# A graph layer with 16 experts on one core: routing by block inside the gather loop, shorter VectorE instructions, and a tail whose second expert row is added by TensorE

## The chip, the cores and the metric

The kernel runs on one core of a Trainium2 chip. A core has five engines that run their own instruction streams and wait for each other by semaphores: TensorE (PE, matmuls; its weight loads are PEld), VectorE (DVE), ScalarE (ACT), GpSimd (POOL) and SyncE (SP, which here only issues DMAs). GpSimd issues the indirect DMAs, those that gather or scatter rows by a list of indices. The metric is the device time of the core in microseconds, lower is better. Before the change it is 911.88 us, the median of three runs of 909.67 to 912.08.

## What is computed

There are 3125 nodes with 256 features and 53125 edges sorted by destination (25000 drawn both ways, and a loop for each node). The reference, cut to what matters:

```python
h = layernorm(x)
agg = segment_sum(h[src], dst, n); deg = segment_sum(1, dst, n)
x = x + h @ W_self + (agg / max(deg, 1)) @ W_neigh + b
xt = layernorm(x)
v, e = top_k(xt @ gate_w + gate_b, 2)         # 16 experts
g = softmax(v)
moe = sum_k g[k] * (relu(xt @ w1[e_k] + b1[e_k]) @ w2[e_k] + b2[e_k])
out = x + layernorm(xt + moe) * gamma + beta
```

Each node picks two of the 16 experts, so 6250 pairs of node and expert are computed. fp32 values that TensorE multiplies are mostly split into two f16 halves (high and low), and three of the four products are taken.

## The kernel before

**Gather loop.** The layer norm h of all nodes is written to DRAM as rows of f16 halves (`h_tab`). The edges are 416 tiles of 128, taken in 26 loop iterations of 16 tiles, each of four quads. GpSimd gathers the source rows of each tile by one indirect DMA (L629) into a ring of 16 slots, and waits ahead of a quad until TensorE is through with the quad four earlier (`quads_done`). For each quad VectorE makes four one-hot matrices of destination against node in one instruction (`onehots`, L1149), and TensorE multiplies them with the gathered rows (L898, L899), two quads to a window of 128 nodes. ScalarE copies the sums out (`row_out`, L769), TensorE turns them (`turn_row`, L904, L905), and VectorE adds them into the node sums `AGG` (`add`, L1190).

**Blocks.** The nodes are 25 blocks of 125. Two iterations behind the edges (LAG = 2) one block per iteration goes through `mean` (L1198 to L1200), the products with W_self and W_neigh on TensorE (`x1_sum`), the layer norm on VectorE (`x1_norm`, L1212 to L1221; its reciprocal root is a chain of small instructions, L427 to L433, each waiting for the one before), the high half on ScalarE (`xt_high`, L759), turning on TensorE (L944), the gate's logits (`gate`), the two largest on VectorE (`gate_out`, L1231 to L1241), and the low half (`xt_low`, L1226). Also in each of the first 16 iterations one expert's W1 and W2 are split into f16 halves, 1024 columns an instruction (ScalarE L783 and L791, VectorE L1260 and L1275). Every engine's stream is written in one fixed order; nothing is scheduled at run time.

**Routing.** Once all blocks are through the loop, VectorE works over all of them at once (L1293 to L1333): one-hots of the chosen experts, a scan that counts each expert's pairs, and each pair's slot, item (tile of 128 pairs of one expert, 64 in all) and row in it; TensorE adds the counts over nodes (L985 to L987) and ScalarE takes the exponent of the softmax. In five chunks VectorE makes one-hots of the item (`eq`, L1338) and of the row (L1340), GpSimd multiplies `eq` by node number and by gate weight (L644, L645), and TensorE's fp32 products (L995) sum them to the lists `tok_of` and `meta_of` (L1347 to L1351).

**Experts.** Then the 64 items run in a pipeline of depth three: GpSimd fetches an item's 128 rows (L657), TensorE turns them (L1006), multiplies with W1 (L1018) and W2 (L1030), VectorE copies both weights to a fixed place (`load_w`, L1366, L1370) and takes the low half of the hidden layer (`split`, L1377), ScalarE copies, takes relu and high half, and scales by the gate weight (`weigh`, L839), and GpSimd scatters the rows to `z_tab` (L663).

**Tail.** In six chunks (2, 4, 6, 6, 4, 3 blocks), pieces of two blocks each: TensorE adds xt, by a product with a diagonal of the standard deviations made on ScalarE (L863, L1070), and b2 by the gate weights (L1071); VectorE adds the two expert rows (L1401), adds TensorE's sum (L1406), and takes moments (L1410, L1415) and centred rows (L1422); GpSimd takes the root (`row_scales`); the output goes out by an accumulating DMA. The last chunk takes its root and its last step (L1426) on VectorE.

## Time and profile before

| | us |
|---|---|
| timed runs | 912.08, 911.88, 909.67 |
| profiled execution, its own time | 907.16 |
| its span in the trace | 905.4 |
| GpSimd busy | 633.6 (70%) |
| TensorE busy | 541.3 (60%) |
| VectorE busy | 537.1 (59%) |
| ScalarE busy | 291.5 (32%) |
| mean granted clock of TensorE | 0.751 |

The span is the time from the first to the last record. The profile names an instruction group by its line, engine and operation, with the tiles it writes and reads (out<-in); "arena", "AGG" and "W" are large blocks of memory of which many tiles are parts, "PS" is the accumulation memory. Behind "|" stand the group's busy time, the mean ns of one, and the idle time of the engine just before them with what ended it; "issue" is time for which the profile shows no wait. The clock is the part of full speed that TensorE was granted; its two levels are 1.2 and 2.4 GHz, so 1.0 is 2.4 GHz.

Mean durations of VectorE's other instructions in the loop, of which the prediction adds up an iteration: an addition (L1190, 384 columns) 555 ns, the reciprocal of `mean` (L1199) 939 ns, its product (L1200) 425 ns, the low half (L1226) 417 ns, the layer norm's wide instructions (L1212, L1215, L1219) 419 to 428 ns and its small ones (L427 to L433) 154 to 164 ns, and those of `gate_out` 168 to 185 ns.

### The profile page before, as it was taken

To read this page: it belongs to the slowest core of one execution; us is meant where nothing else is said; L and a number is where in the kernel's file an instruction comes from. 1 tells how busy PE (TensorE), PEld (TensorE's weight loads), DVE (VectorE), ACT (ScalarE), POOL (GpSimd) and SP (SyncE) were. 2 spreads that over 40 slices of the span, in tenths; PEclk is the share of its full clock that TensorE was granted. 3 is DMA by queue.
4 is the path that set the end of the run, shared out by engine and by line. 5 is a ranking of instruction groups with operands and counts; after the bars stand their busy time and mean duration, and the time that the engine had idled before them with its cause. 6 is when DMAs were issued, how large, how long until landed. Compare 5 with 4: busy or idle time off the path is not lost.

```text
span 905.4 us, 15122 instructions
## 1 busy us (share of the span) xinstructions
PE 541.3 (60%) x4348; PEld 435.3 (48%) x4348; DVE 537.1 (59%) x1386; ACT 291.5 (32%) x688; POOL 633.6 (70%) x657
## 2 busy tenths in 40 slices
PE   0034565565565664646556556632789999999720
PEld 0022443444343443434434444421689999998610
DVE  7622356666556666564554554468577777777296
ACT  5311111112211121100110000010188999988621
POOL 6377777777777777777777777505757777776265
PEclk9995566656666667576676677555799999999965
DMA  8544555566555555544444444310133223222897
GB/s 192 166 151 147 156 166 178 166 185 186 178 176 172 169 174 168 155 130 122 128 128 128 122 127 127 108 30 22 35 87 93 91 90 93 72 88 65 190 228 115
DMA packets 65021, 120.09 MB, mean 133 GB/s; under 512 B 11645, under 2 KB 39469, under 8 KB 64970
## 3 DMA queue, kind: packets, MB, share of 16 engines
q0 software_dynamic: 29088, 72.17, 28.4%
q1 hardware_dynamic: 35734, 46.86, 18.4%
q8 instruction: 26, 0.43, 0.2%
q10 hardware_dynamic: 148, 0.43, 0.2%
q14 instruction: 25, 0.20, 0.1%
HBM read 100.21 MB, written 21.19 MB: 134 GB/s over the span
## 4 chain that ended last, share of the span: by engine, by line
POOL 45%; PE 23%; issue 15%; DMA 8%; DVE 7%; SPq 1%; ACT 0%; DVEq 0%; ACTq 0%; POOLq 0%
POOL arena L629 42%; PE PS L1018 9%; PE PS L1030 9%; DMA arena<-h_tab,arena 4%; PE PS L1006 1%; DMA W<-z_tab 1%; DMA arena<-xh_tab,tok_of 1%; PE PS L995 1%; PE PS L898 1%; DMA W<-in_x 1%; DVE W L1422 1%; PE PS L899 1%; POOL AGG L644 1%; DVE W L1406 1%; DMA z_tab<-arena,meta_of 1%
## 5 line engine op out<-in xcount | busy, mean ns | idle before, releaser
L629 POOL DMA_INDIRECT arena<-h_tab,arena x416 | 412.7, 992 | 138.6 <-issue 124.3
L898 PE MATMUL PS<-arena 128*128 128x257 f16 x416 | 142.4, 358 | 214.6 <-DMA arena<-h_tab,arena 214.4
L898 PEld LDWEIGHTS PS<-arena 128*128 128x128 f16 x416 | 51.2, 123 | 253.6 <-issue 183.6
L899 PE MATMUL PS<-arena 128*128 128x256 f16 x416 | 145.3, 364 | 0.0
L1190 DVE TENSOR_TENSOR AGG<-AGG,PS 128x384 f32 x52 | 28.9, 555 | 124.5 <-PE PS L905 118.9
L1018 PE MATMUL PS<-arena,AGG 128*128 128x128 f16 x1536 | 97.5, 221 | 1.6 <-DVE AGG L1366 1.6
L1149 DVE TENSOR_TENSOR arena<-iota,arena 128x512 f16<-128x512 f16 x104 | 70.2, 690 | 45.3 <-PE PS L899 37.0
L1030 PE MATMUL PS<-AGG,arena 128*128 128x256 f16 x768 | 95.8, 273 | 0.2 <-DVE arena L1377 0.2
L759 ACT ACTIVATE arena<-arena 125x256 f16<-125x256 f32 x25 | 10.4, 417 | 256.3 <-DVE arena L1219 256.3
L769 ACT ACTIVATE arena<-PS 128x257 f32<-128x257 f32 x52 | 19.8, 380 | 226.9 <-PE PS L899 226.9
L663 POOL DMA_INDIRECT z_tab<-arena,meta_of x64 | 69.7, 1090 | 31.7 <-issue 19.0
L1018 PEld LDWEIGHTS PS<-arena,AGG 128*128 128x128 f16 x1536 | 89.8, 99 | 1.8 <-DVE AGG L1366 1.8
L657 POOL DMA_INDIRECT arena<-xh_tab,tok_of x64 | 74.9, 1170 | 22.5 <-ACT arena L839 13.4
L1030 PEld LDWEIGHTS PS<-AGG,arena 128*128 128x128 f16 x768 | 72.5, 98 | 9.2 <-issue 0.5
L823 ACT ACTIVATE arena<-PS,arena 128x128 f32<-128x128 f32 x256 | 73.0, 368 | 5.9 <-PE PS L1018 3.6
L1377 DVE TENSOR_TENSOR arena<-arena 128x512 f16<-128x512 f32 x64 | 44.3, 692 | 46.6 <-ACT arena L832 46.6
L899 PEld LDWEIGHTS PS<-arena 128*128 128x128 f16 x416 | 51.4, 123 | 13.4
L832 ACT ACTIVATE arena<-arena 128x512 f16<-128x512 f32 x64 | 40.3, 630 | 16.0 <-PE PS L1030 15.8
L1366 DVE COPY AGG<-W 128x2048 f16 x64 | 44.7, 699 | 0.3 <-issue 0.3
L1370 DVE COPY AGG<-W 128x2048 f16 x64 | 44.9, 702 | 0.0
L815 ACT ACTIVATE arena<-PS 128x512 f16<-128x512 f16 x64 | 37.6, 587 | 5.5 <-PE PS L1006 5.5
L944 PE MATMUL PS<-ident,arena 125*128 125x125 f32 x50 | 16.7, 438 | 37.3 <-DVE arena L1219 37.2
(208 smaller groups left out, 971.4 us busy)
## 6 DMA issues: line engine op xcount, KB each, us to landing
W<-in_L_ffn_w SPq DMA_DIRECT2D x31, 512.0 KB, 4.0
arena<-h_tab,arena POOLq DMA_INDIRECT x416, 3.0
arena<-h_tab SPq DMA_DIRECT2D x25, 125.0 KB
arena<-in_x SPq DMA_DIRECT2D x25, 125.0 KB
out<-arena SPq DMA_DIRECT2D x25, 125.0 KB
xh_tab<-arena SPq DMA_DIRECT2D x25, 125.0 KB
W<-z_tab SPq DMA_DIRECT2D x2, 1344.0 KB
W<-z_tab SPq DMA_DIRECT2D x2, 896.0 KB
```

Of the source, the lines that this page charges most:

```text
L629: g.indirect_dma_start(msg[:, s, u, 0:2 * D], None, h_tab[:, :], bass.IndirectOffsetOnAxis(ap=srcT[:, t:t + 1], axis=0)).then_inc(gathered ...
L657: g.indirect_dma_start(xsr[:, n % 4, :].bitcast(f16), None, xh_tab[:, :], bass.IndirectOffsetOnAxis(ap=tok_of[:, n:n + 1], axis=0)).then_i ...
L663: g.indirect_dma_start(z_tab[:, :], bass.IndirectOffsetOnAxis(ap=meta_of[:, n, 0:1].bitcast(i32), axis=0), yo[:, n % 4, :], None, bounds_c ...
L823: ins = a.activation(hr[:, s % 2, c * P:(c + 1) * P], p_h[s % 2][:, c * P:(c + 1) * P], ACT.Relu, bias=b1e[:, s % 2, c:c + 1], scale=1.0 / ...
L898: t.matmul(p, oh[:, h, u, :], msg[:, s, u, D:2 * D + 1], start=first, stop=False)
L899: return t.matmul(p[:, 0:D], oh[:, h, u, :], msg[:, s, u, 0:D], start=False, stop=last)
L1018: ins = t.matmul(p_h[s % 2][:, c * P:(c + 1) * P], w1e[:, s % 2, wa, k, c * P:(c + 1) * P], xT[:, s % 2, xa, k, :], start=(y == 0), stop=( ...
L1030: ins = t.matmul(p_y[s % 2], h[:, s % 2, c * P:(c + 1) * P], w2e[:, s, wa, c, :], start=(y == 0), stop=(y == len(terms) - 1))
L1149: v.tensor_tensor(oh[:, h, :, :], iota16[:, :].unsqueeze(1).to_broadcast([P, QT, P]), relT[:, bass.ds(TPR * r + QT * h, QT)].unsqueeze(2). ...
L1366: v.tensor_copy(w1e[:, s % 2, :, :, :].rearrange("p a k f -> p (a k f)"), W1[:, bass.ds(e, 1), :, :, :].rearrange("p e a k f -> p (e a k f ...
L1370: v.tensor_copy(w2e[:, s, :, :, :].rearrange("p a c d -> p (a c d)"), W2[:, bass.ds(e, 1), :, :, :].rearrange("p e a c d -> p (e a c d)")) ...
L1377: v.tensor_tensor(hl[:, s % 2, :], hr[:, s % 2, :], hh[:, s % 2, :], ALU.subtract).then_inc(h_split, 1)
```

## The change

1. **Short instructions.** The one-hots of a quad are four instructions of 128 columns with the destination as a scalar per row. The weights' low halves are made in four pieces each.
2. **Routing by block.** In the loop, behind `gate_out`, a new `pick` makes the one-hots of the block's two experts; TensorE (`place`) counts each pair's place among its expert's pairs, from the block and a running count; a new `place_rows` on VectorE makes of it the row one-hots of the block's pairs, once times the place of the node within its block (`row_tok`) and once times the block's number (`row_blk`), in f16. The loop is staged anew (`place_rows` three iterations behind the mean), the root of `x1_norm` is shortened to nine linked instructions on a column (`rsqrt_column`), and TensorE's node products are parted in two (own, neighbours).
3. **The last iteration** is written out apart and the last blocks have second buffers for the rows, turned rows and logits, and block 23 goes through its norm, gate and pick between the last quads' steps.
4. **Routing's end.** With the tiles of each expert known, the pairs' items are found by one product and one sum over the experts (L1485, L1486); five `eq` of 640 elements follow; TensorE makes the lists by 200 f16 products (two for each half block) and VectorE puts both together (L1500 to L1505). GpSimd has no part in it.
5. **Gate weights.** The rows that go to `z_tab` are not scaled any more. All factors are left as a ratio e1 to the first expert's weight; the norm's eps is scaled along (`epsr`). `gate_rows` (VectorE, ahead of the fourth item's weight copy) and `gate_low` make the factors for b2 and xt while the experts run.
6. **The tail.** VectorE makes the diagonals of xt once TensorE is through with the experts, ScalarE those of the ratio (`diag_r`), and TensorE adds the second expert's rows by fp32 products with them (`second_expert`), with the products of xt and b2 six pieces ahead. VectorE's addition of the two rows goes.

The order of VectorE's stream at three places. First, behind the last block's mean; before (block 24, numbered from 0):

```order
L1200 TENSOR_TENSOR arena<-AGG,arena 128x250 [waits deg_step]
L1226 TENSOR_TENSOR arena<-arena 125x256 [waits xt_hi]
L1285 TENSOR_SCALAR AGG<-iota 128x25 [waits mean_made]
L1286 MEMSET AGG 125x400
L1287 MEMSET AGG 125x16 [waits dve_step]
L1231 TENSOR_TENSOR lg<-PS,gb_b 125x16 [waits logits,dve_step]
L1235 MAX m<-lg 125x8 [waits logits_out,top_out]
L1238 MAX_INDEX i<-m,lg 125x8 [waits top_step]
L1239 COPY val<-m 125x2
L1241 CAST idxf<-i 125x2 [waits top_step]
L1212 SCALAR_TENSOR_TENSOR arena<-PS,arena 125x256 [waits xx_stored,hxx_loaded,x1_summed]
```
and with the change:

```order
L1308 TENSOR_TENSOR arena<-AGG,arena 128x250 [waits deg_step]
L1380 TENSOR_TENSOR arena<-AGG,PS 125x32 [waits ohs_made,pos_made]
L1382 TENSOR_TENSOR cum<-cum,ohs 125x16 [waits place_step]
L1383 TENSOR_REDUCE arena<-arena 125x2
L1384 CAST arena<-arena 125x2 [waits place_step]
L1385 TENSOR_SCALAR arena<-arena 125x2 [waits place_step]
L1386 CAST AGG<-arena 125x2 [waits place_step]
L1389 TENSOR_SCALAR arena<-arena 125x1 [waits place_step,cols_made]
L1390 SCALAR_TENSOR_TENSOR arena<-AGG,arena 125x2 [waits place_step]
L1393 TENSOR_SCALAR AGG<-iota,arena,tok 125x128 [waits place_step]
L1393 TENSOR_SCALAR AGG<-iota,arena,tok 125x128
L1396 TENSOR_SCALAR AGG<-iota,arena 125x128 x2
```
Before, the low half and the first rows of the routing over all blocks follow, and then the gate of block 23. Now the 11 instructions of `place_rows` for block 22 stand between the mean and the norm of block 24, and block 23's gate is ahead of the mean.

Second, in the chunks of the routing's end, `eq` and row one-hots before (L1338, L1340):

```order
L1340 TENSOR_TENSOR arena<-iota,AGG 125x1280
L1338 TENSOR_TENSOR AGG<-iota,AGG 125x640 [waits pv_made]
L1340 TENSOR_TENSOR arena<-iota,AGG 125x1280
L1338 TENSOR_TENSOR AGG<-iota,AGG 125x640 [waits pv_made]
L1340 TENSOR_TENSOR arena<-iota,AGG 125x1280
L1347 TENSOR_SCALAR tok_of<-PS 128x64 [waits chunk_done]
L1348 TENSOR_SCALAR tok_of<-tok_of 128x64 [waits dve_step]
```
and with the change (L1490 is `eq`):

```order
L1490 TENSOR_TENSOR arena<-iota,arena 125x640 [waits dve_step]
L1493 TENSOR_SCALAR arena<-arena,iotap 128x16
L1494 TENSOR_REDUCE arena<-arena 128x1 [waits dve_step]
L1495 TENSOR_SCALAR arena<-arena 128x1 [waits dve_step]
L1490 TENSOR_TENSOR arena<-iota,arena 125x640 x3
L1498 CAST items<-PS 1x64 [waits item_T]
L1490 TENSOR_TENSOR arena<-iota,arena 125x640
L1500 COPY arena<-PS 128x64 [waits chunk_done]
L1501 SCALAR_TENSOR_TENSOR arena<-PS,arena 128x64 [waits dve_step]
L1502 TENSOR_SCALAR tok_of<-arena 128x64 [waits dve_step]
```
The waits for GpSimd's products (`pv_made`) and the row one-hots of 1280 elements are gone; the small steps behind the sums are more.

Third, in the experts, from the second item's `split` on; before:

```order
L1377 TENSOR_TENSOR arena<-arena 128x512 [waits hi_split]
L1362 TENSOR_LOAD items
L1362 ISA x2
L1365 ISA [waits relu_done,l1_done]
L1365 COPY arena<-b1T 128x4
L1366 ISA
L1366 COPY AGG<-W 128x2048
```
and with the change, where `gate_rows` (L1513 to L1522) comes ahead of the fourth item's weights (L1537):

```order
L1552 TENSOR_TENSOR arena<-arena 128x512 [waits hi_split]
L1513 MEMSET arena 125x1200 [waits xh_stored,xx_stored,ratio_made]
L1514 TENSOR_SCALAR AGG<-AGG 125x25x16
L1515 SCALAR_TENSOR_TENSOR AGG<-AGG,ratio 125x25x16
L1517 TENSOR_TENSOR arena<-AGG 125x25x16 [waits gates_summed]
L1518 TENSOR_SCALAR epsr<-ratio 125x25
L1519 TENSOR_TENSOR rstds<-rstds,epsr 125x25 [waits gates_summed]
L1520 TENSOR_SCALAR arena<-rstds 125x25 [waits gates_summed]
L1522 SCALAR_TENSOR_TENSOR epsr<-epsr 125x25 [waits g3_zeroed]
L1537 TENSOR_LOAD items
```
Eight instructions have been put ahead of the copies of the fourth item's weights, and the first of them waits for ScalarE's ratio and for stores.

The diff, cut to its core:

```diff
+        def rsqrt_column(v, link, var, vs, t, y):
+
+            link(v.scalar_tensor_tensor(vs, quads[0:BT, :], var, quads_eps[0:BT, :], ALU.mult, ALU.add))
+            link(v.tensor_scalar(t.bitcast(i32), vs[:, 0:1].bitcast(i32), 1, None, ALU.logical_shift_right))
+            link(v.tensor_scalar(y.bitcast(i32), t.bitcast(i32), -1.0, float(0x5F3759DF) - 2.0 ** 31, ALU.mult, ALU.add))
+            for c in range(3):
+                link(v.scalar_tensor_tensor(t, y, vs[:, c:c + 1], y, ALU.mult, ALU.mult))
+                link(v.scalar_tensor_tensor(y, t, 3.0, y, ALU.subtract, ALU.mult))
...
-                g.tensor_tensor(pv[c % 2][:, :, 0, :], eq[c % 2], tok1[:, js].unsqueeze(2).to_broadcast([BT, CH, NITEM]), ALU.mult).then_inc(pv_made, 1)
-                g.tensor_tensor(pv[c % 2][:, :, 1, :], eq[c % 2], wts[:, js].unsqueeze(2).to_broadcast([BT, CH, NITEM]), ALU.mult).then_inc(pv_made, 1)
...
+            def place(j):
+
+                pe.wait_ge(ohs_made, j + 1)
+                pe.wait_ge(cum_made, j + 1)
+                t.matmul(p_pos[in_end(j)], lower16[:, :], ohs[is_last(j)][:, :], start=True, stop=False)
+                t.matmul(p_pos[in_end(j)], ones16[0:BT, 0:BT], cum[:, :], start=False, stop=True).then_inc(pos_made, 1)
...
-                pe.wait_ge(oh_row_made, c + 1)
-                pe.wait_ge(pv_made, 2 * (c + 1))
-                for j in range(CH):
-                    ins = t.matmul(p_meta, oh_row[:, c * CH + j, :], pv[c % 2][:, j, :, :],
-                                   start=(c == 0 and j == 0), stop=(c == NG - 1 and j == CH - 1))
+                pe.wait_ge(eq_made, c + 1)
+                for j in range(c * CH, (c + 1) * CH):
+                    b, k = divmod(j, 2)
+                    t.matmul(p_tok, row_tok[:, b, k, :], eq[:, j, :], start=(j == 0), stop=(j == BK - 1))
+                    ins = t.matmul(p_blk, row_blk[:, b, k, :], eq[:, j, :], start=(j == 0), stop=(j == BK - 1))
...
+            def second_expert(i):
+
+                lo, hi = PIECES[i]
+                pe.wait_ge(diag_r_made, i + 1)
+                pe.wait_ge(z_loaded[CHUNK_OF[i]], 2 * DMA)
+                for b in range(lo, hi):
+                    ins = t.matmul(p_sum[i % 8][:, b - lo, :], diag_r[:, b, :], Z[0:BT, b, 1, :], start=False, stop=(b == hi - 1))
                 ins.then_inc(p_made, 1)
+
+            for i in range(AHEAD):
+                residual(i)
+            for i in range(len(PIECES)):
+                second_expert(i)
+                if i + AHEAD < len(PIECES):
+                    residual(i + AHEAD)
...
-                v.tensor_tensor(oh[:, h, :, :], iota16[:, :].unsqueeze(1).to_broadcast([P, QT, P]),
-                                relT[:, bass.ds(TPR * r + QT * h, QT)].unsqueeze(2).to_broadcast([P, QT, P]),
-                                ALU.is_equal).then_inc(signal, 1)
+                for u in range(QT):
+                    ins = v.tensor_scalar(oh[:, h, u, :], iota16[:, :], relT[:, bass.ds(TPR * r + QT * h + u, 1)], None, ALU.is_equal)
+                ins.then_inc(signal, 1)
...
+                link(v.tensor_tensor(o, iota16[0:BT, 0:NEXP].unsqueeze(1).to_broadcast([BT, 2, NEXP]),
+                                     idx2[:, :].unsqueeze(2).to_broadcast([BT, 2, NEXP]), ALU.is_equal), alone=True)
+                v.tensor_tensor(ohs[is_last(j)][:, :], o[:, 0, :], o[:, 1, :], ALU.add).then_inc(ohs_made, 1)
...
+            def place_rows(j):
+
+                link, n = counted_link(dve, place_step, PLACE_STEPS * j)
+                o = oh2[:, bass.ds(j, 1), :].rearrange("p b (k e) -> p (b k) e", k=2)
+                t2 = tiles[:, bass.ds(j, 1), :].rearrange("p b k -> p (b k)")
+                dve.wait_ge(pos_made, j + 1)
+                dve.wait_ge(ohs_made, j + 1)
+                link(v.tensor_tensor(picked[:, :, :], o, p_pos[in_end(j)].unsqueeze(1).to_broadcast([BT, 2, NEXP]), ALU.mult), alone=True)
+                if not is_last(j):
+                    v.tensor_tensor(cum[:, :], cum[:, :], ohs[0][:, :], ALU.add).then_inc(cum_made, 1)
+                link(v.tensor_reduce(pos2[:, :], picked[:, :, :], AX.X, ALU.add))
+                link(v.tensor_copy(tile2[:, :], pos2[:, :]))
+                link(v.tensor_scalar(tile2[:, :], tile2[:, :], P.bit_length() - 1, None, ALU.logical_shift_right))
+                link(v.tensor_copy(t2, tile2[:, :]))
+                dve.wait_ge(cols_made, j + 1)
+                carry(dve)
+                link(v.tensor_scalar(block1[:, :], block1[:, :], 1.0, None, ALU.add))
+                link(v.scalar_tensor_tensor(row2[:, :], t2, -float(P), pos2[:, :], ALU.mult, ALU.add), alone=True)
+                assert n[0] == PLACE_STEPS
+                for k in range(2):
+                    v.tensor_scalar(row_tok[:, bass.ds(j, 1), k, :].rearrange("p b c -> p (b c)"), iota16[0:BT, :],
+                                    row2[:, k:k + 1], tok2[:, k:k + 1], ALU.is_equal, ALU.mult)
+                for k in range(2):
+                    ins = v.tensor_scalar(row_blk[:, bass.ds(j, 1), k, :].rearrange("p b c -> p (b c)"), iota16[0:BT, :],
+                                          row2[:, k:k + 1], block1[:, 0:1], ALU.is_equal, ALU.mult)
+                ins.then_inc(cols_made, 1)
...
-                        v.scalar_tensor_tensor(w[:, 1, :], wstg1, WS1, w[:, 0, :], ALU.mult, ALU.subtract).then_inc(w1_lo, 1)
+                        for c in range(4):
+                            cs = slice(c * KC * F // 4, (c + 1) * KC * F // 4)
+                            ins = v.scalar_tensor_tensor(w[:, 1, cs], wstg1[:, cs], WS1, w[:, 0, cs], ALU.mult, ALU.subtract)
...
+            xt_low(NB - 3)
+            x1_norm(NB - 2)
+            place_rows(NB - 4)
+            add(LAST, 0)
+            gate_out(NB - 3)
+            pick(NB - 3)
+            last_base = row_base(2 * LAST + 1)
+            add(LAST, 1, last_base)
             dve.wait_ge(adds_done, ER + 2)
             mean(NB - 1)
+            place_rows(NB - 3)
+            x1_norm(NB - 1)
             xt_low(NB - 2)
...
+            gate_out(NB - 2)
+            pick(NB - 2)
+            gate_out(NB - 1)
+            pick(NB - 1)
+            place_rows(NB - 2)
+            xt_low(NB - 1)
+            dve.wait_ge(top_out, 2 * NB + 2)
...
+            link(v.tensor_tensor(at_e, ohf, tile0[0:BT, :].unsqueeze(1).unsqueeze(1).to_broadcast([BT, NB, 2, NEXP]), ALU.mult))
+            link(v.tensor_reduce(itemf.rearrange("p (b k) -> p b k", k=2), at_e, AX.X, ALU.add))
...
+                v.memset(G3, 0.0).then_inc(g3_zeroed, 1)
+                v.tensor_scalar(pairs[:, :, 0, :], ohf[:, :, 0, :], WS2, None, ALU.mult)
+                link(v.scalar_tensor_tensor(pairs[:, :, 1, :], ohf[:, :, 1, :], WS2, ratio[:, :].unsqueeze(2).to_broadcast([BT, NB, NEXP]),
+                                            ALU.mult, ALU.mult))
+                v.tensor_tensor(gates[:, :, 0:NEXP], pairs[:, :, 0, :], pairs[:, :, 1, :], ALU.add)
+                link(v.tensor_scalar(epsr[:, :], ratio[:, :], 1.0, WS2, ALU.add, ALU.mult))
+                link(v.tensor_tensor(rstds[:, :], rstds[:, :], epsr[:, :], ALU.mult))
+                v.tensor_scalar(gates[:, :, NEXP], rstds[:, :], -1.0, None, ALU.mult)
...
+            for lo, hi in PIECES:
+                for b in range(lo, hi):
+                    ins = v.tensor_scalar(diag[:, b, :], ident[0:BT, 0:BT], rstds[:, b:b + 1], None, ALU.mult)
...
-                link(v.tensor_tensor(z[:, :, 0, :], z[:, :, 0, :], z[:, :, 1, :], ALU.add))
...
```
## Rows read from the trace of the kernel before

**Rows 1.** Stretches; from:to, length, busy of PE, PEld, DVE, ACT, POOL (instructions), clock, DMA, GB/s.
```profile
41.86:582.90 541.04, 301.81 (x1512) 217.21 (x1513) 283.11 (x823) 78.52 (x152) 412.68 (x416) 0.67 0.52 153
582.90:652.80 69.90, 31.39 (x166) 26.73 (x167) 48.14 (x115) 5.37 (x11) 27.89 (x19) 0.62 0.09 26
652.80:844.00 191.20, 187.54 (x2558) 175.87 (x2556) 134.36 (x253) 167.08 (x446) 139.75 (x123) 0.99 0.31 88
```

**Rows 2.** Costliest groups of the page, the gather.
```profile
L629 POOL DMA_INDIRECT arena<-h_tab,arena x416 | 412.7, 992 | 138.6 <-issue 124.3
```

**Rows 3.** The gather's line: ns least/median/most, first and last start.
```profile
L629 POOL DMA_INDIRECT arena<-h_tab,arena x416: 942/946/1897, 41.9 to 580.0; - x139
```

**Rows 4.** Timeline in the gather; start us, duration us, engine, line.
```profile
453.00 1.30 DVE L1149 TENSOR_TENSOR arena<-iota,arena 128x512 f16<-128x512 f16 x2 [0.34 <-issue]
453.12 1.39 POOL L629 DMA_INDIRECT arena<-h_tab,arena  x1 [0.30 <-issue]
```

**Rows 5.** Timeline from the last gather to the first fetch.
```profile
580.03 0.95 POOL L629 DMA_INDIRECT arena<-h_tab,arena  x1 [0.30 <-issue]
...
582.90 0.38 PE L898 MATMUL PS<-arena 128*128 128x257 f16 x1 [1.82 <-DMA arena<-h_tab,arena]
...
608.93 0.98 DVE L1294 TENSOR_TENSOR AGG<-iota,idxf 125x800 f32<-125x800 f16 x1
...
620.21 0.82 DVE L1338 TENSOR_TENSOR AGG<-iota,AGG 125x640 f32<-125x640 f16 x1
...
647.80 0.99 POOL L657 DMA_INDIRECT arena<-xh_tab,tok_of  x1 [1.10 <-DVE tok_of L1348]
```

**Rows 6.** Groups by line, VectorE, 41.86 to 582.9 us.
```profile
L1149 DVE TENSOR_TENSOR arena<-iota,arena 128x512 f16<-128x512 f16 x102 | 68.9, 691 | 43.4 <-PE PS L899 37.0 <-issue 5.5
...
L1275 DVE SCALAR_TENSOR_TENSOR W<-W 128x1024 f32 (+1 forms) x15 | 18.3, 1218 | 0.0
...
L1221 DVE TENSOR_TENSOR arena<-arena,beta_b 125x256 f32<-125x256 f32 x23 | 9.9, 430 | 0.8
...
L1198 DVE TENSOR_SCALAR arena<-AGG 128x125 f32 (+1 forms) x24 | 6.0, 250 | 3.9 <-DVE AGG L1190 3.8
```

**Rows 7.** Timeline of VectorE, last block.
```profile
595.35 0.23 DVE L1198 TENSOR_SCALAR arena<-AGG 128x125 f32<-128x125 f32 x1
...
596.70 0.42 DVE L1200 TENSOR_TENSOR arena<-AGG,arena 128x250 f32<-128x250 f32 x1
...
601.13 0.43 DVE L1212 SCALAR_TENSOR_TENSOR arena<-PS,arena 125x256 f32<-125x256 f32 x1
...
604.81 0.15 DVE L1218 COPY rstds<-arena 125x1 f32<-125x1 f32 x1
605.00 0.41 DVE L1219 TENSOR_SCALAR arena<-arena 125x256 f32<-125x256 f32 x1
```

**Rows 8.** Timeline in and behind the experts.
```profile
659.17 1.01 PE L1018 MATMUL PS<-arena,AGG 128*128 128x128 f16 x15 [1.59 <-DVE AGG L1366]
...
699.27 1.23 POOL L657 DMA_INDIRECT arena<-xh_tab,tok_of  x1 [0.31 <-ACT arena L839]
...
699.68 0.69 DVE L1366 COPY AGG<-W 128x2048 f16 x1
...
843.86 1.54 PE L1053 MATMUL PS<-ident,AGG 125*96 125x125 f16 x25
```

**Rows 9.** Groups by line, VectorE, 851 to 905.4 us.
```profile
L1401 DVE TENSOR_TENSOR W<-W 125x1024 f32<-125x1024 f32 (+3 forms) x6 | 7.6, 1265 | 14.1 <-DMA W<-z_tab 14.1
```

**Rows 10.** Timeline of the tail, TensorE and VectorE.
```profile
864.73 1.06 PE L1070 MATMUL PS<-W,AGG 125*125 125x256 f32 x2
...
866.64 1.76 DVE L1401 TENSOR_TENSOR W<-W 125x1536 f32<-125x1536 f32 x1 [0.16 <-DMA W<-z_tab]
...
875.37 1.75 DVE L1401 TENSOR_TENSOR W<-W 125x1536 f32<-125x1536 f32 x1
```

**Rows 11.** Groups by line, VectorE, 653 to 844 us.
```profile
L1370 DVE COPY AGG<-W 128x2048 f16 x63 | 44.1, 700 | 0.0
```

579 lines of the change are left out of this document (332 added, 247 removed).

## The prediction

> **What bounds the kernel now.** I read the stretches first, then the costliest groups, then the order of time at each seam. The stretches [rows 1] part the span of 905.4 us. From 41.9 to 582.9 us the edges are gathered: GpSimd is busy 412.7 of 541 us, no other engine over 302. From 582.9 to 652.8 the routing runs, 69.9 us with every engine mostly idle: a chain from engine to engine. From 652.8 to 844.0 the 64 items of the experts run with TensorE busy 187.5 of 191.2 us at the high clock. What is left, 61.4 us, is the tail (DMA, then VectorE).
>
> In the gather GpSimd is the bound by itself: 416 gathers, least 942 ns, median 946, mean 992, and gaps put down to "issue" of 124.3 us, 0.30 each [rows 2 to 4]. An undisturbed gather is 0.945 + 0.300 = 1.245 us, a loop iteration of 16 is 19.9 us, and 415 steps are 517 us; the rest up to the last start at 580.03 [rows 5] is 416 x (0.992 - 0.946) = 19.1 us of lengthened gathers, plus 2. What lengthens them stands in [rows 4]: a gather that begins at 453.12, while VectorE's one-hot of 453.00 is running, takes 1.39 us: it waits until about 0.12 us before that instruction's end at 453.69. The row of 453.00 holds two one-hots back to back; the gather waits only for the first, so the wait ends between them.
>
> **The gather, part by part.** The one-hot of 512 columns (102 x 0.691 us, two tensor inputs) becomes four of 128 with a column scalar; a weight split of 1024 columns (30 x 1.218, two lines with x15 each) becomes four of 256 [rows 6]. A gather that starts inside an instruction of length L waits on average (L - 0.12)^2 / 2L. Before: 70 us of one-hots meet 70/1.3 = 54 starts x 0.235 = 13; 37 us of splits meet 28 x 0.495 = 14; together 27, where the rows show 19, so I scale by 0.7. After: the nearest row for 128 columns is 0.25 us (x24), for 256 columns 0.43 (x23) [rows 6]: 104 us at most in 80 starts x 0.034 = 2.7, and 42 us in 33 x 0.11 = 3.7, scaled 4.5. The new per-block instructions are as short; I add 1.5. So 6 of 19 stay: **13 us gained** (5 to 19, no less than the scaling doubled, no more than all of it).
>
> This holds only while VectorE keeps up. A full iteration on it, by start-to-start spacing: four one-hot groups 2.8 (4 x 0.17 each), two additions 1.6, mean 1.8 (595.35 to 597.12 [rows 7]), low half 0.4, layer norm 4.1 (601.13 to 605.41 is 4.3, less three linked steps of 0.19, as between 604.81 and 605.00, plus 0.43 for the beta row [rows 6, 7]), gate and pick 1.9, place_rows 2.3 (seven linked steps, four instructions of at most 0.25), weight splits 8 x 0.34 = 2.7: 17.6 of 19.9 us, and without weights 15. Before it was busy 283 of 541 us [rows 1], which leaves out the gaps of its linked steps. TensorE's new waits (place for the pick) stand a whole iteration behind in the loop, and GpSimd waits for a quad only four quads later, some 9 us of slack. So the new work is hidden there; without that cover it would be 2.7 us x 20 iterations.
>
> **The bridge.** Four pieces, from the last gather's landing (582.90, TensorE's first matmul on it [rows 5]) to the first fetch (647.80).
> 1. To the last mean: before 596.70 + 0.42 - 582.90 = 14.2 us [rows 7]. After, VectorE's queue in the last iteration decides. From about 8.3 us after the first of its four landings (TensorE is through with own and neighbour products and the second quad at 8.7) it has: norm of block 22 4.1, one-hot 0.7, gate and pick 1.6, low half 0.4, norm of 23 4.1, place_rows 2.1, addition 0.8, gate and pick 1.6, addition 0.9, mean 1.8 = 18.1, so the mean is there at 26.4 to 27.2, and the last landing is at 15: 12.0. Gain 2.
> 2. Mean to normalized rows of block 24: before 597.12 to 605.41 = 8.3 [rows 7]. After place_rows of 22 (2.1) and a norm of 3.5: 5.8. Gain 2.5.
> 3. From there to the first routing instruction over all blocks at 608.93 it was 3.5. Now: row tail 0.6, two low halves 0.8, two gates and picks 3.1, the difference 0.2, two place_rows 4.2 = 8.9. Loss 5.4. Then 608.93 to 620.21 was 11.3 [rows 5]; its successor is five small steps at 0.21, two of 800 elements at 0.98 (the row of 608.93 has 800) and one of 0.2: 3.3. Gain 8.
> 4. The five chunks: 620.21 to 647.80 = 27.6 us [rows 5], in which GpSimd's products and VectorE's comparisons take turns. After, GpSimd has none of it; the five comparisons of 640 elements take at most 0.82 each, as the one of 620.21 did before GpSimd began, and TensorE's 200 matmuls follow. I count 100 pairs as two instructions that hide each other's loads half: 0.062 us for one at the high clock (25 in 1.54 us [rows 8]), twice that at the low one, so 6.2 to 25 us; TensorE starts low (0.62 in this stretch [rows 1]). I take 9 for all of them, plus 0.7 ahead and 1.0 of small steps behind: 10.7. Gain 17 (2 to 20).
> Sum: 2 + 2.5 - 5.4 + 8 + 17 = 24; I take **23.5 us** (bounds 9 to 29). The 5.0 us from fetch to first matmul stay.
>
> **The experts.** TensorE, the bound, has the same instructions. New is gate_rows in VectorE's queue ahead of the weight copy for item 3: a memset of 1200 words (1.3 us by the 0.82 of 640 elements), three of 400 elements (0.5 each) and four small ones (0.2): 3.6 us. VectorE has 134 us of work in 191 [rows 1] and catches up later, but at the start TensorE already waits for just such a copy (659.17, 1.59 us [rows 8]). I put 3 of it on the path; ScalarE's two copies (1.0 us), on an engine busy 167 of 191 us [rows 1], add 0.5: **3.5 lost** (1 to 6).
>
> **The tail.** VectorE's additions of the second row go: 6, 7.6 us busy [rows 9]; from 866.64 on it was the bound [rows 10]. In their place each piece of two blocks needs two fp32 products on TensorE before VectorE may add: 0.85 us a block at the low clock (1.06 with the overlap of its two passes [rows 10]), half at the high one, and the residual of six pieces ahead (0.55, or 1.06, a block) stands between them. VectorE needs 2.3 us per piece (a chunk of three from 866.64 to 875.37 is 8.73, less the 1.76 that go [rows 10]), TensorE 2.0 at the high clock and 4.1 at the low one, until the residuals are through. Walking the chunks gives 2 us gained at the high and 5 lost at the low clock; the last chunk's own steps stay. I take **1 gained** (7.6 gained to 5 lost). The 25 diagonals (4.8 us on VectorE) lie under the wait for the z table (most of 14.1 us [rows 9]).
>
> **Sum.** -13 - 23.5 + 3.5 - 1 = -34.0. The profiled execution took 907.16 us (span 905.4), so 873.2 by its own time; the median of the timed runs is 4.7 above it, and by that 877.9. I forecast **878**.
>
> **Rivals.**
> A. The seam is longer than my walk: TensorE's small matmuls at the low clock throughout take 20 instead of 9 us, or the last iteration's queue slips by one norm. For it: every engine's work there is in one order with waits in both directions, and the clock was 0.62 [rows 1]. Against: TensorE has work without gaps in the chunks, and such work ran at the high clock in the experts [rows 1]. Price 11: 889.
> B. All of it pays: 18 of the gather's 19 us, chunks in 7.5, the tail's 7.6 less 1. For it: two-input instructions are the only ones that I find before long gathers. Price: -5 - 1.5 - 5.6: 866.
> C. **VectorE becomes the bound of the gather** (slower). Place: the loop's 24 new short instructions. If each has to wait for GpSimd's port and stands 0.36 us instead of 0.17, the iteration needs 17.6 + 24 x 0.19 = 22.2 us. It decides from 19.9 on, and the gain of the other parts (21 us) is gone when 20 iterations exceed that by 2.0 each, 21.9. At 22.2 the loop is 46 us over its floor, where before it was 19: 911.9 - 21 + 27 = 918. Against it: VectorE's copies of 2048 columns average 0.700 us x63 [rows 11] while GpSimd's descriptors are written in 73% of the time (139.75 of 191.2 us [rows 1]), and the gather at 699.27 is what waits (1.23 us) behind the copy of 699.68 [rows 8].
> The Trainium skill, "SBUF — State Buffer", section "Who interferes with whom", speaks for C: a one-source instruction such as tensor_scalar or copy can enter a two-port mode and then it and a GpSimd instruction block each other, whoever starts first, whereas tensor_tensor only meets GpSimd's reads. By that rule the change swaps a weak contender for a strong one. The trace agrees that the copy holds GpSimd up in mid-instruction, and shows no wait of VectorE.
> D. The short instructions free nothing, the lengthened gathers staying at 19 us: 891 with the rest as forecast. Against: the wait ends with the first of two back-to-back instructions [rows 4].
>
> **Chances.** Forecast (870 to 885) 0.55; A 0.15; B 0.14; D 0.08; C 0.06; the rest, a miss in both gather and bridge that ends within a few us of no change, 0.02. Range 864 to 894: it leaves out C, the far end of A and the far end of B; the forecast's own range is 870 to 885. Within 0.3% (2.7 us) is about what a measurement cannot tell from no change. Faster 0.92, same 0.02, slower 0.06.
>
> **What would show it.** Gather: mean of the 416 near 0.96 us, last start near 567, few over 1.2. Bridge: 46 us from last landing to first expert matmul, with the last mean 12 us in, and GpSimd idle. Experts: one TensorE wait of about 3 us near the third item, then 2.9 us each. Tail: no addition of the second row, VectorE waiting on TensorE in several pieces. It would be wrong if GpSimd waits for TensorE in the loop (C), if the gathers keep their 0.992 mean (D), or if the small matmuls take over 15 us (A).

## The result, and the profile after

The changed kernel takes 888.80 us, the median of 4 runs (886.31 to 889.21), against 911.98 us of the kernel before (909.67 to 912.34, 4 runs): a ratio of 0.9752, 95% interval 0.9734 to 0.9769. That is 23.2 us faster, where 33.9 were forecast. The profiled execution took 888.89 us, its span is 887.1 us, 18.3 under the span before; the profiled execution before was 4.8 us under its own median, and in which stretch these 4.8 us lie no trace shows.

By stretch, each from the two traces (forecast in the last column):

| stretch | before | after | change | forecast |
|---|---|---|---|---|
| start to first gather | 41.86 | 43.29 | +1.4 | 0 |
| first to last gather start | 538.17 | 535.88 | -2.3 | -13 |
| last gather to first fetch | 67.77 | 46.83 | -20.9 | -23.5 |
| first fetch to first W1 product | 5.02 | 4.95 | -0.1 | 0 |
| first W1 product to end of last W2 product | 191.20 | 195.08 | +3.9 | +3.5 |
| from there to the end | 61.3 | 61.1 | -0.3 | -1 |

The first row is no part of the change: kernels with the same start had their first gather at 41.3 to 42.5 us. The stretches of the changed kernel (from:to, length, busy time and instructions of PE, PEld, DVE, ACT and POOL, clock, DMA share, GB/s) stand against [rows 1]:

```profile
43.29:582.10 538.81, 292.66 (x1551) 227.88 (x1552) 344.00 (x1450) 78.34 (x151) 410.39 (x416) 0.71 0.51 154
582.10:630.95 48.85, 21.72 (x177) 17.86 (x178) 35.12 (x140) 4.60 (x10) 4.03 (x4) 0.53 0.12 35
630.95:826.02 195.07, 188.68 (x2557) 175.65 (x2556) 137.59 (x262) 162.11 (x448) 140.81 (x124) 0.99 0.29 87
```

GpSimd is almost idle in the second (4.03 of 48.9 us, was 27.9 of 69.9), and in the first it is as busy as before: 410.4 against 412.7 us. The gather's line, which answers to [rows 3], says where that comes from (ns least/median/most):

```profile
L677 POOL DMA_INDIRECT arena<-h_tab,arena x416: 942/946/3239, 43.3 to 579.2; - x139
```

The median is the same, but the longest gather now takes 3.24 us, before 1.90. Of the 416, six take over 1.5 us. Summed over all gathers, what each takes over 0.945 us is 19.6 us before and 17.3 after. Sorted by what VectorE was doing when a lengthened gather began (the instruction begun last, if it was still running), in us, with the gathers lengthened by over 0.02 us and all that began there:

| VectorE at the gather's start | before | after |
|---|---|---|
| one-hot, two inputs (before) or scalar (after) | 10.25 (38 of 52) | 0.24 (7 of 54) |
| weights' low halves | 8.1 (18 of 29) | 13.0 (22 of 26) |
| other two-input instructions | 0.6 | 3.4 |

Of the 14 that began in a two-input one-hot and were not lengthened, 11 began in its last 0.15 us, where the gather gets in at once; so did all 11 not lengthened in the low halves before. So the one-hots gave what was forecast and more, and the weights' low halves, cut in four, and the other two-input instructions took it back. The timeline shows how; the first of the six long gathers (start us, duration us):

```profile
67.39 0.95 POOL L677 DMA_INDIRECT arena<-h_tab,arena  x1 [0.30 <-issue]
67.70 0.24 DVE L1253 TENSOR_SCALAR arena<-iota,arena 128x128 f16<-128x128 f16 x1
67.87 1.42 DVE L1426 SCALAR_TENSOR_TENSOR W<-W 128x256 f16<-128x256 f32 x4
68.65 2.80 POOL L677 DMA_INDIRECT arena<-h_tab,arena  x1 [0.30 <-issue]
69.21 1.42 DVE L1432 SCALAR_TENSOR_TENSOR W<-W 128x256 f16<-128x256 f32 x4
71.75 0.95 POOL L677 DMA_INDIRECT arena<-h_tab,arena  x1 [0.30 <-issue]
```

The gather of 68.65 begins while the third of the first four pieces runs. If it waited for that piece alone it would be lengthened by 0.2 us, as with the one-hots in [rows 4]. It is held through the rest of L1426 and all four pieces of L1432, to 70.51, 0.12 us before their end at 70.63, and then takes its 0.945: 2.80 us. The eight pieces follow each other every 0.335 us; the waits for ScalarE's high halves, ahead of the first and the fifth, had long been met and held nothing up. The six long gathers stand in iterations 0 to 4 and 15, the ones whose weight part is written out for one iteration; in the ten iterations that run as a loop (5 to 14) the gathers beside the same pieces are lengthened by 0.27 us at most. Four of the kernels below leave this part of the loop as it is (`gate_rows`, the last quad, both of the tail), and their traces say the same: in each of iterations 0 to 4 a gather is held until 0.12 us before the row's end, 25 of 25 with the changed kernel, and in 50 loop iterations none is. A gather that began 0.08 us ahead of the first piece, in the last scalar one-hot, was held longest (with `gate_rows` moved):

```profile
156.58 0.74 DVE L1253 TENSOR_SCALAR arena<-iota,arena 128x128 f16<-128x128 f16 x4 [2.19 <-PE PS L935]
157.16 3.66 POOL L677 DMA_INDIRECT arena<-h_tab,arena  x1 [0.30 <-issue]
157.24 1.42 DVE L1426 SCALAR_TENSOR_TENSOR W<-W 128x256 f16<-128x256 f32 x4
158.58 1.42 DVE L1432 SCALAR_TENSOR_TENSOR W<-W 128x256 f16<-128x256 f32 x4
```

Iteration 15, with one row of four pieces, is mixed: held to the row's end in three of the five, but in the kernel with the last quad ahead a gather that began in the first piece got in at that piece's end:

```profile
380.95 1.43 DVE L1439 SCALAR_TENSOR_TENSOR W<-W 128x256 f16<-128x256 f32 x4
381.08 1.11 POOL L677 DMA_INDIRECT arena<-h_tab,arena  x1 [0.30 <-issue]
```

### The profile page after: what moved, and what is told of

The parts are those of the page before. It is cut to its first block, busy times and chain, and to the rows that moved or that the text cites. A ratio compares the mean times of both kernels' runs of the same rounds, so it can differ in the third digit from the quotient of the medians.

```text
span 887.1 us, 16659 instructions
## 1 busy us (share of the span) xinstructions
PE 535.8 (60%) x4447; PEld 446.4 (50%) x4447; DVE 586.1 (66%) x2080; ACT 285.5 (32%) x688; POOL 602.5 (68%) x643
## 3 DMA queue, kind: packets, MB, share of 16 engines
q1 hardware_dynamic: 35734, 46.86, 18.3%
## 4 chain that ended last, share of the span: by engine, by line
POOL 45%; PE 20%; issue 17%; DVE 8%; DMA 8%; SPq 1%; ACT 0%; DVEq 0%; ACTq 0%; POOLq 0%
POOL arena L677 43%; PE PS L1103 8%; PE PS L1115 8%; DMA arena<-h_tab,arena 2%; DMA arena<-xh_tab,tok_of 2%; DMA W<-z_tab 1%; PE PS L1091 1%; DMA W<-in_x 1%; POOL arena L685 1%; DVE W L1604 1%; DMA z_tab<-arena,meta_of 1%; PE PS L934 1%; DVE arena L1592 1%; PE PS L935 1%; POOL W L638 1%
## 5 line engine op out<-in xcount | busy, mean ns | idle before, releaser
L677 POOL DMA_INDIRECT arena<-h_tab,arena x416 | 410.4, 987 | 138.5 <-issue 124.0
L934 PE MATMUL PS<-arena 128*128 128x257 f16 x416 | 145.8, 364 | 249.2 <-DMA arena<-h_tab,arena 249.1
L1253 DVE TENSOR_SCALAR arena<-iota,arena 128x128 f16<-128x128 f16 x416 | 80.2, 272 | 114.3 <-PE PS L935 111.4
L935 PE MATMUL PS<-arena 128*128 128x256 f16 x416 | 148.5, 370 | 0.0
L685 POOL DMA_INDIRECT arena<-xh_tab,tok_of x64 | 72.7, 1136 | 67.6 <-DVE tok_of L1503 45.9
L691 POOL DMA_INDIRECT z_tab<-arena,meta_of x64 | 73.9, 1154 | 34.0 <-ACT arena L869 18.6
L792 ACT ACTIVATE arena<-PS 128x250 f32<-128x250 f32 x25 | 9.5, 378 | 179.0 <-PE PS L991 179.0
L971 PE MATMUL PS<-ws,arena 128*125 128x256 f16 x150 | 35.5, 404 | 0.0
```

The costliest lines, as they stand in the source:

```text
L677: g.indirect_dma_start(msg[:, s, u, 0:2 * D], None, h_tab[:, :], bass.IndirectOffsetOnAxis(ap=srcT[:, t:t + 1], axis=0)).then_inc(gathered ...
L685: g.indirect_dma_start(xsr[:, n % 4, :].bitcast(f16), None, xh_tab[:, :], bass.IndirectOffsetOnAxis(ap=tok_of[:, n:n + 1], axis=0)).then_i ...
L691: g.indirect_dma_start(z_tab[:, :], bass.IndirectOffsetOnAxis(ap=meta_of[:, n:n + 1], axis=0), yo[:, n % 4, :], None, bounds_check=2 * N - ...
L934: t.matmul(p, oh[:, h, u, :], msg[:, s, u, D:2 * D + 1], start=first, stop=False)
L935: return t.matmul(p[:, 0:D], oh[:, h, u, :], msg[:, s, u, 0:D], start=False, stop=last)
L1253: ins = v.tensor_scalar(oh[:, h, u, :], iota16[:, :], relT[:, bass.ds(TPR * r + QT * h + u, 1)], None, ALU.is_equal)
```

## The experiments

Each kernel was timed in turns with the kernel before, and not with the changed kernel. Before's time was 910.97 us beside whole instructions, linked pieces and the two forms of two-input one-hots, 908.17 beside one wait ahead, `gate_rows`, the last quad and the tail by chunk, and 910.05 beside the other four; beside the changed kernel it was 911.98. The totals are set against the changed kernel's 888.80 all the same, so a difference of under about 4 us between two of them shows nothing by itself, and the stretches of the traces decide. The ratio to the kernel before, 0.9752 for the changed kernel, stands with each. "Lengthening" is the sum over the 416 gathers of what each took over 0.945 us; "loop" is first to last gather start.

### The rows of pieces: four kernels

**Whole instructions again.**

```diff
-for c in range(4):
-    ins = v.scalar_tensor_tensor(w[:, 1, cs], wstg1[:, cs], WS1, w[:, 0, cs], ALU.mult, ALU.subtract)
-ins.then_inc(w1_lo, 1)
+v.scalar_tensor_tensor(w[:, 1, :], wstg1, WS1, w[:, 0, :], ALU.mult, ALU.subtract).then_inc(w1_lo, 1)
```

(and so for W2.)

> The changed kernel, with the low halves of the weights made by one instruction of 1024 columns again instead of four of 256. Theory run: VectorE instructions with two tensor inputs that follow each other without a semaphore wait between them hold the gathers up until the last of them is nearly done, so four pieces in a row count as one long instruction (12 gathers of the changed kernel's trace, 1.3 to 2.3 us longer each, 12 us in all, stand behind such rows of pieces). Then one long instruction costs the same as four pieces: 887 to 891 us, and again some 12 gathers of over 2 us. Theory length: each instruction holds by itself, so the pieces did help and the long ones must come from elsewhere; then this is 5 to 8 us slower, 894 to 897 us.

Measured: 887.16 us (883.49 to 888.84), ratio 0.9722, lengthening 17.1, loop 535.7. The longest gather takes 3.18 us; ten take over 1.5. Cutting an instruction of 1024 columns in four gained nothing in sum, as theory run has it: the two whole instructions, now one behind the other, also hold as one in four of the first five iterations. (The changed kernel's trace has six gathers held by a row, 10.6 us together, and not the 12 that theory run sets out from.) The sum hides two parts. In the ten loop iterations, where nothing holds as one, the pieces lengthen gathers by 2.4 us and the whole instructions by 5.0; in the six written out it is 10.6 against 8.2.

**Pieces linked by waits.**

```diff
+plink, _ = counted_link(dve, piece_step, 6 * i)
 for c in range(4):
     ins = v.scalar_tensor_tensor(w[:, 1, cs], wstg1[:, cs], WS1, w[:, 0, cs], ALU.mult, ALU.subtract)
+    if c < 3:
+        plink(ins)
```

> The changed kernel, with each piece of a weight's low half waiting by a semaphore for the piece before it. Theory run: the row of pieces is broken, a gather waits for one piece of 0.4 us at most, and of the 13 us of lengthening behind pieces (12 gathers) 2 to 3 stay: 878 to 881 us, no gather over 1.5 us behind a split. Theory length: nothing changes, 889, or a little slower by the added waits of VectorE.

Measured: 877.02 us (874.66 to 878.72), ratio 0.9618, 11.8 us under the changed kernel; lengthening 5.6, loop 524.2, 11.7 shorter:

```profile
L678 POOL DMA_INDIRECT arena<-h_tab,arena x416: 942/946/1337, 42.4 to 566.6; - x139
```

With a wait of each piece for the one before it no gather takes over 1.34 us. The whole difference in time is the difference in lengthening.

**One wait ahead of the pieces.** The pieces are as in the changed kernel; VectorE only waits for its own last one-hot first.

```diff
 if weights == "both":
+    dve.wait_ge(oh_ready, QR * i + 6)
     dve.wait_ge(w1_hi, i + 1)
```

> The changed kernel, with one wait of VectorE for its own last one-hot ahead of the first piece of the weights' low halves; the pieces themselves follow each other without waits as in the changed kernel. Theory entered (in the changed kernel the row of pieces stands behind one-hots with a column scalar; with two-input one-hots in their place no gather was held over 1.5 us, so it is the passage from the one-hots into the pieces that leaves the hold in place): the wait breaks the passage, no gather over 1.5 us, 877 to 880 us. Theory pieces (a row of pieces holds whatever stands ahead of it): as the changed kernel, 886 to 890 us, 6 or more gathers over 1.5 us.

Measured: 879.58 us (879.21 to 880.29), ratio 0.9682, lengthening 6.2, loop 524.8, no gather over 1.28 us. The same place in its timeline:

```profile
64.85 0.66 DVE L1253 TENSOR_SCALAR arena<-iota,arena 128x128 f16<-128x128 f16 x3
65.54 1.43 DVE L1427 SCALAR_TENSOR_TENSOR W<-W 128x256 f16<-128x256 f32 x4
65.79 1.00 POOL L677 DMA_INDIRECT arena<-h_tab,arena  x1 [0.30 <-issue]
66.89 1.42 DVE L1433 SCALAR_TENSOR_TENSOR W<-W 128x256 f16<-128x256 f32 x4
67.09 1.03 POOL L677 DMA_INDIRECT arena<-h_tab,arena  x1 [0.30 <-issue]
```

Two gathers begin inside rows of pieces that run as closely as before, and each gets in at the end of the piece that it met (1.00 and 1.03 us). So theory pieces, by which a row of pieces holds whatever stands ahead of it, fell. What counts is how VectorE comes into the row. It takes a wait for VectorE's own last instruction: the wait for ScalarE's high half stood ahead of the row in the changed kernel too and did not help. In iterations 0 to 4 the row starts 0.03 us behind the last one-hot's end with its own wait, and 0.08 us ahead of that end without it.

Where in the row a gather begins does not explain it. In iterations 0 to 4 the held ones of the changed kernel began 0.34 to 1.04 us behind the row's start; with the wait they began at 0.22 to 0.25 and 1.09, with the four two-input one-hots below at 0.39 to 1.01, and none was held past its piece.

**Whole instructions with the wait ahead** (both edits above).

> The changed kernel, with the weights' low halves in one instruction of 1024 columns each and the wait ahead of them. Theory entered (the hold that outlasts an instruction is what the wait mends; the length of each instruction then counts by itself): a gather that starts in one is held at most 1.1 us, some 10 to 20 of the 31 instructions are hit for 0.5 us each, so 5 to 9 us over the kernel with pieces and the wait (879.6): 884 to 888. If the wait alone is all that matters: 879 to 881.

Measured: 885.40 us (883.56 to 889.22), ratio 0.9728, lengthening 13.8, longest gather 1.98. The hold is back to one instruction (1.98 is 1.04 + 0.945), and with the way in mended, length does count: 13.8 against 6.2 us. So with the wait the pieces are worth 7.6 us (the loop is 532.4 us against 524.8), where without it they were worth nothing in sum.

### The one-hots: three kernels

**One instruction with two inputs again.**

```diff
-for u in range(QT):
-    ins = v.tensor_scalar(oh[:, h, u, :], iota16[:, :], relT[:, bass.ds(TPR * r + QT * h + u, 1)], None, ALU.is_equal)
-ins.then_inc(signal, 1)
+v.tensor_tensor(oh[:, h, :, :], iota16[:, :].unsqueeze(1).to_broadcast([P, QT, P]),
+                relT[:, bass.ds(TPR * r + QT * h, QT)].unsqueeze(2).to_broadcast([P, QT, P]),
+                ALU.is_equal).then_inc(signal, 1)
```

> The changed kernel, with the one-hots of a quad in one instruction of 512 columns with two tensor inputs again. Both theories: the gathers that start inside it are lengthened as in the kernel before (35 gathers, 10.2 us there): 897 to 901 us, gather mean 1.00 to 1.02 us. A third theory, that the form of the one-hots never mattered and the order of the stream is what counts, gives 889.

Measured: 890.58 us (885.90 to 894.37), ratio 0.9768, lengthening 19.1: only 1.8 slower, where both theories had 8 or more. The sum is nearly the same, its parts are not: 51 gathers behind one-hots make 14.4 us, and the low halves make 2.7 us, with no gather over 1.5. The long holds are gone without any edit of the pieces. This miss led to the experiment with the wait ahead.

**Four instructions with two inputs.**

```diff
-    ins = v.tensor_scalar(oh[:, h, u, :], iota16[:, :], relT[:, bass.ds(TPR * r + QT * h + u, 1)], None, ALU.is_equal)
+    ins = v.tensor_tensor(oh[:, h, u, :], iota16[:, :],
+                          relT[:, bass.ds(TPR * r + QT * h + u, 1)].to_broadcast([P, P]), ALU.is_equal)
```

> The changed kernel, with the four one-hots of a quad as four instructions of 128 columns, but with two tensor inputs each (tensor against tensor, the scalar column stretched) and no wait between them. Theory run: they hold as one instruction of 0.7 us, as slow as the single one of 512 columns (897 to 901 us). Theory length: four short holds of 0.17 us, 1 to 3 us over the changed kernel: 890 to 892 us. Theory scalar form irrelevant: 889.

Measured: 880.12 us (877.72 to 882.35), ratio 0.9653, 8.7 faster than with the scalar form, which no theory had. Lengthening is 9.1: 36 of 72 gathers begun in one-hots make 4.0 us, against 0.24 for the scalar form, and the low halves make 2.8 against 13.0. Four short two-input instructions without a wait do not hold as one, so theory run is wrong in its general form. The three forms also part the one-hots' gain: 14.4 us in one instruction, 4.0 in four with two inputs, 0.24 in four with a scalar. So length gave most of it and the form the rest. Its timeline at the low halves:

```profile
86.88 1.42 DVE L1427 SCALAR_TENSOR_TENSOR W<-W 128x256 f16<-128x256 f32 x4
87.68 1.10 POOL L677 DMA_INDIRECT arena<-h_tab,arena  x1 [0.30 <-issue]
88.22 1.42 DVE L1433 SCALAR_TENSOR_TENSOR W<-W 128x256 f16<-128x256 f32 x4
89.08 1.04 POOL L677 DMA_INDIRECT arena<-h_tab,arena  x1 [0.30 <-issue]
```

The same rows of pieces, entered from two-input one-hots with no wait, let each gather in at the next boundary.

**The kernel before with scalar one-hots only** (the first diff of this group, the other way, in the kernel before).

> The kernel before, with only the one-hots changed: four instructions of 128 columns with a column scalar instead of one of 512 with two tensor inputs. In its trace the gathers behind one-hots are lengthened by some 10 us. Theory length: nearly all of this goes, 8 to 10 us below the kernel before in the same rounds. Theory entered: the one-hots stand ahead of the low half of W1 here too, and the hold passes on into it in some iterations, so 4 to 8 us below.

Measured: 904.19 us (901.70 to 906.07) against 910.05, ratio 0.9930 (0.9909 to 0.9951): 5.9 us faster. Lengthening 14.8, 14 gathers over 1.5 us, the longest 1.92, all of them beside an instruction of 1024 columns. Gathers begun in one-hots make 0.3 us (9 of 51 lengthened) against 10.25, but those begun in the low halves 13.3 (26 of 31) against 8.1 (18 of 29). The gain is within theory entered's numbers, but not by its mechanism: no gather there is held past one instruction. The low halves of W1 and W2 stand apart in it, and only two of its iterations are written out, so it could hardly show the long hold. About as many gathers meet the low halves as before, but earlier in them: 11 of the 29 had begun in the last 0.15 us, now 5 of 31. Before, a gather held by the one-hot ahead put the next one just at the low half's end, so in 10 of 16 iterations:

```profile
193.03 1.42 POOL L629 DMA_INDIRECT arena<-h_tab,arena  x1 [0.30 <-issue]
193.55 1.22 DVE L1260 SCALAR_TENSOR_TENSOR W<-W 128x1024 f32 x1
194.75 0.95 POOL L629 DMA_INDIRECT arena<-h_tab,arena  x1 [0.30 <-issue]
```

So a hold that is taken away moves the gathers behind it, and some of them meet the next long instruction worse.

### The three other terms

**gate_rows where VectorE is idle.**

```diff
-dve_step_of(n)
-if n == -1:
-    gate_rows()
+if n == -2:
+    run_item(load_w, n, 3, None)
+    gate_rows()
+    run_item(split, n, 2, None)
+else:
+    dve_step_of(n)
```

> The changed kernel, with gate_rows put between the second item's weight copies and the first item's split, where VectorE stands idle for 4.63 us, instead of ahead of the fourth item's weight copies. Theory queue (the 3.9 us that the experts grew come from TensorE waiting for copies queued behind gate_rows): TensorE's wait of 2.71 us goes, first up product to last down product 195.1 us becomes 191.2 to 192, total 3 to 4 us less: 885. Theory other (the growth is from ScalarE's two copies or from GpSimd): at most 1 us less.

Measured: 882.91 us (881.87 to 888.30), ratio 0.9740, experts 190.54 us (195.08). In the changed kernel TensorE stands twice for weight copies in the first items:

```profile
637.29 1.51 PE L1103 MATMUL PS<-arena,AGG 128*128 128x128 f16 x24 [1.27 <-DVE AGG L1541]
...
643.07 1.51 PE L1103 MATMUL PS<-arena,AGG 128*128 128x128 f16 x24 [2.71 <-DVE AGG L1541]
```

and in this one only once, then 2.9 us an item from the third:

```profile
635.46 1.51 PE L1103 MATMUL PS<-arena,AGG 128*128 128x128 f16 x24 [1.03 <-DVE AGG L1541]
...
638.37 1.50 PE L1103 MATMUL PS<-arena,AGG 128*128 128x128 f16 x24
```

Theory queue holds; ScalarE's two copies cost nothing that shows. (The ten kernels with `gate_rows` where the change has it spread from 193.6 to 197.2 us in this stretch; the two with it moved have 190.5 and 192.2.)

**The last quad ahead of block 22's logits.**

```diff
-gate(NB - 3)
 quad(LAST, 3)
 turn(LAST, 1)
+gate(NB - 3)
```

> The changed kernel, with TensorE taking the last quad and its turn ahead of the logits of block 22 instead of behind them. In the changed kernel's trace TensorE stands 5.4 us for these logits, whose memory is freed by VectorE's place_rows, with the last quad landed. Theory TensorE's order: VectorE no longer waits 0.65 and 1.74 us around the last addition, last mean 2 to 2.5 us earlier, last gather to first fetch 46.8 us becomes 44.5, total 886 to 887. Theory VectorE's order (VectorE's own queue sets the end of the loop): under 0.7 us less.

Measured: 885.43 us (885.09 to 886.16), ratio 0.9749; last gather to first fetch 44.54 us (46.83), 2.3 shorter. In the changed kernel:

```profile
591.24 0.99 PE L1003 MATMUL PS<-gw,arena 128*125 128x16 f32 x4 [5.42 <-DVE AGG L1396]
592.07 0.38 PE L934 MATMUL PS<-arena 128*128 128x257 f16 x1
...
595.67 0.55 DVE L1297 TENSOR_TENSOR AGG<-AGG,PS 128x384 f32 x1 [1.74 <-PE PS L941]
...
597.61 0.42 DVE L1308 TENSOR_TENSOR arena<-AGG,arena 128x250 f32<-128x250 f32 x1
```

The logits wait 5.42 us for the last instruction of `place_rows` (L1396), and the last quad, landed near 582, queues behind them until 592.07. With the two swapped:

```profile
582.55 0.42 PE L934 MATMUL PS<-arena 128*128 128x257 f16 x1
...
587.88 0.99 PE L1003 MATMUL PS<-gw,arena 128*125 128x16 f32 x4 [2.46 <-DVE AGG L1396]
...
591.23 0.55 DVE L1297 TENSOR_TENSOR AGG<-AGG,PS 128x384 f32 x1 [0.67 <-issue]
...
593.16 0.42 DVE L1308 TENSOR_TENSOR arena<-AGG,arena 128x250 f32<-128x250 f32 x1
```

VectorE's wait for the turned sums (1.74 us) is gone. Against the last gather, which starts at 576.12 here and at 579.17 in the changed kernel, the last mean's product is 1.4 us earlier (17.04 against 18.44 us behind it). The other 0.9 us lie further on and were not traced: kernels with an unchanged seam have 45.7 to 47.6 us there. So the swap is worth 1.4 to 2.3 us. The total's 3.4 is not a measure of it: this execution also has its first gather 1.7 us earlier, a loop 1.4 shorter (534.5 us) and a tail 1.9 longer.

**The tail by chunk.**

```diff
-for i in range(len(PIECES)):
-    second_expert(i)
-    if i + AHEAD < len(PIECES):
-        residual(i + AHEAD)
+for q in range(NT):
+    of_q = [i for i in range(len(PIECES)) if CHUNK_OF[i] == q]
+    for i in of_q:
+        second_expert(i)
+    for i in of_q:
+        if i + AHEAD < len(PIECES):
+            residual(i + AHEAD)
```

> The changed kernel, with TensorE adding the second expert's rows of all pieces of a chunk before it goes on with the products of xt and b2 for later pieces. Theory TensorE's order (in the third chunk of the tail VectorE waits 1.3 to 1.9 us for TensorE, which has products for later pieces between): last down product to end 61.1 us becomes 59 to 60. Theory loads (the later chunks wait for the z rows to land, 0.7 to 2.2 us each): no change, 60.8 to 61.3 us.

Measured: 887.63 us (886.79 to 889.71), ratio 0.9776, tail 61.3 us: no change. In the changed kernel TensorE waits for z rows in the later chunks (L1164 is the second expert's product), and here it does too:

```profile
849.56 1.10 PE L1164 MATMUL PS<-W,AGG 125*125 125x256 f32 x4 [0.80 <-DMA W<-z_tab]
...
856.34 1.10 PE L1164 MATMUL PS<-W,AGG 125*125 125x256 f32 x4 [0.68 <-DMA W<-z_tab]
...
860.63 1.96 PE L1164 MATMUL PS<-W,AGG 125*125 125x256 f32 x8 [0.93 <-DMA W<-z_tab]
...
864.83 1.53 PE L1164 MATMUL PS<-W,AGG 125*125 125x256 f32 x6 [2.23 <-DMA W<-z_tab]
```

```profile
857.44 2.83 PE L1164 MATMUL PS<-W,AGG 125*125 125x256 f32 x12 [1.05 <-DMA W<-z_tab]
...
862.39 1.96 PE L1164 MATMUL PS<-W,AGG 125*125 125x256 f32 x8 [1.58 <-DMA W<-z_tab]
...
865.77 1.53 PE L1164 MATMUL PS<-W,AGG 125*125 125x256 f32 x6 [1.42 <-DMA W<-z_tab]
```

This is what theory loads has: the chunks' products start when their rows have landed, and the order of TensorE's products between them made no difference that shows.

**The addition on VectorE again.**

```diff
-ins = t.matmul(p_sum[i % 8][:, b - lo, :], diag_r[:, b, :], Z[0:BT, b, 1, :], start=False, stop=(b == hi - 1))
...
 dve.wait_ge(z_loaded[q], 2 * DMA)
+link(v.tensor_tensor(z[:, :, 0, :], z[:, :, 0, :], z[:, :, 1, :], ALU.add))
```

> The changed kernel with the tail's second row added by VectorE again (one addition for each chunk; the ratio is left out, so the rows are added unscaled) and without the fp32 products of the second row on TensorE and their diagonals on ScalarE. Theory traded: what the additions cost in the last three chunks (3.9 us) is set against what TensorE's products and the loads cost in the third (2.1 us), so 1 to 2 us slower than the changed kernel, tail 62 to 63 us against 61.1. Theory loads (the landing of z sets the tail either way): equal within 0.5 us. Theory gain lost: the VectorE form is faster by 1 us or more.

Measured: 888.11 us (886.92 to 890.83), ratio 0.9759, tail 62.0 us. The total is 0.7 under the changed kernel, the tail 1.0 over it, and the tail alone spreads from 60.4 to 63.0 us over the ten kernels that have it in the changed form. So the swap is worth less than this spread of 2.6 us either way, and which way is not shown. Here too VectorE waits for the z rows ahead of its additions (7.09, 0.76 and 0.39 us).

### The three mends together

> The changed kernel with three edits together: pieces of the weights' low halves linked by waits, gate_rows in VectorE's idle time, and the last quad ahead of block 22's logits. If the causes are separate, the gains add: 877.0 for the linked pieces, less 4 for gate_rows and 2.3 for the last quad: 870 to 872 us. If the last quad or gate_rows hid behind the lengthened gathers, less than that: 874 to 877.

Measured: 871.63 us (870.50 to 871.88), ratio to the kernel before 0.9568 (0.9551 to 0.9584). The gains add up within the noise (877.0 less 4 and 2.3 is 870.7). It is 17.2 us under the changed kernel, and by its span 17.3: 12.4 in the loop (lengthening 4.9), 2.9 in the experts (192.2), 1.0 from last gather to fetch (45.8) and 1.0 ahead of the first gather, which no edit touched. So the last quad's 1.4 to 2.3 us did not fully come back here: 45.8 lies within the 45.7 to 47.6 of kernels without the swap.

## Why the prediction was right and wrong

- **The gather, the step that failed.** The term of the sum was 13 us gained; it was 2.3. The one-hot's part came as priced and better, from 10.25 to 0.24 us, but not by length alone, by which it was worked out: with two inputs and the same length 4.0 us stay. What failed is "42 us in 33 x 0.11 = 3.7", the estimate for the cut weight splits, which takes each instruction of length L by itself. The low halves hold 13.0 us, more than the 8.1 before, because in six iterations one gather waits for the whole row. The other new instructions hold 3.4, where 1.5 was added. Linking the pieces (-11.7 us of loop) and the single wait ahead (-11.1) both give it back; with either, lengthening is 5.6 to 6.2 us, which is the "6 of 19" of the forecast.
- **Rivals C and D.** C, VectorE as the bound of the gather, did not come: GpSimd waits for TensorE 2.4 us in all, VectorE is busy 344 of 538.8 us, and a scalar one-hot lengthened only 7 of 54 gathers, by 0.24 us. The Trainium skill, "SBUF — State Buffer", section "Who interferes with whom", has copies and tensor_scalar in a two-port mode as the ones that shut GpSimd out, and two-input instructions as contending with GpSimd's reads, though not as stalling a DMA. In the traces the two-input instructions do stall GpSimd's gathers (37 of the 40 that began in a one-hot before its last 0.15 us waited), so the measurement decides against that last point; whether it is a read that waits no run shows. Of the first the changed kernel's trace shows almost nothing for gathers begun in a scalar one-hot, and whether that instruction ran in such a mode no trace tells. But the long holds came only with scalar one-hots right ahead of the row, so the form does matter for what comes behind it. A, a longer seam by slow matmuls, did not come, though its condition did: the granted clock was 0.53 from the first comparison at 617.78 to 624.79, when the sums were read, 7.0 us later. The lists take 100 products and not the 200 of the prediction and of the list of changes (50 half blocks, two each), and back to back they follow each other every 0.053 us at the low clock, where 0.124 had been taken (the duration in these rows overlaps with the next one's):

```profile
617.78:624.79 7.01, 5.55 (x101) 5.32 (x101) 4.35 (x9) 0.00 (x0) 0.00 (x0) 0.53 0.01 2
L1079 PE MATMUL PS<-arena,AGG x50: 193/242/243, 619.4 to 624.5; 125*128 125x64 f16 x50
L1080 PE MATMUL PS<-arena,AGG x50: 193/242/242, 619.4 to 624.6; 125*128 125x64 f16 x50
```

B, all of it paying, was off by the gather. D named the outcome, the mean staying at 0.99 us (it is 0.987), at 891 us against 888.8; its reason, that short instructions free nothing, is wrong: what the one-hots freed, the rows took.
- **The bridge.** 20.9 us against 23.5. The chunks gave 19.4 (27.6 became 8.2, from 617.78 to the fetch at 626.00) where 17 were taken; half as many products as had been counted is part of it. Routing ahead of them took 12.7 us where 12.2 had been worked out (`place_rows` has 12 instructions and not 11). The normalization of block 24 gave 1.2 instead of 2.5. The last mean, forecast 2 us earlier, came 1.8 later (16 us behind the last landing, taken 2.87 us behind the last gather's start as in [rows 5], not 12): the walk had TensorE "through with own and neighbour products and the second quad at 8.7", and left out that the logits wait for `place_rows` with the last quad behind them. Swapping them gave 1.4 to 2.3 us back in one kernel, 1.0 at most in the one with all three edits.
- **The experts.** 3.9 us against 3.5, and the cause as named: with `gate_rows` moved it is gone. Its instructions took 3.0 us on VectorE (638.66 to 641.64), where 3.6 were added up.
- **The tail.** 0.3 us gained where 1 was taken, within the bounds. But the same tail spreads by 2.6 us from kernel to kernel, so 0.3 is not told from nothing, and that the term fits is no proof of it. The clock that the step turned on was at both levels: four products of the second row took 2.04 us at first and 1.03 later.

```profile
842.99 2.04 PE L1164 MATMUL PS<-W,AGG 125*125 125x256 f32 x4 [0.89 <-DMA W<-z_tab]
846.64 1.03 PE L1164 MATMUL PS<-W,AGG 125*125 125x256 f32 x4
```

The landing of the z rows, which the step had only ahead of the first chunk, held TensorE in the later ones as well (4.6 us in the four waits shown above). What sets the tail's length was not settled.
- **The sum.** Between the profiled executions the forecast was 15.7 us too low (873.2 against 888.89): 10.7 in the gather, 2.6 in the bridge, 1.4 ahead of the first gather, 1 in experts and tail. By the medians it is 10.8 us, since the profiled execution before was 4.8 us under its median and the one after was not. The forecast's own range, 870 to 885, did not hold the time; the stated range of 864 to 894 did because it reached as far as D, whose reason is wrong. That it was right is luck in this part.

## What to carry to other kernels

When GpSimd issues the gathers that bound a loop, look for gathers over the median and at the VectorE instruction in which each began. Two-input instructions cost them the rest of their own length; cutting long ones short is worth it only if the row of pieces does not hold as one. A wait of VectorE for its own last instruction, ahead of the row or in it, kept that from happening in every iteration here. In the row it made the loop iterations' eight pieces 4.3 us long, before 2.8, which VectorE had to spare. Then look again, for every hold that goes moves the gathers behind it. And where work is moved from behind a loop into its last iteration, walk the queue of each engine that the moved instruction's waits can stop, for what stands behind it: here a 16-column product held up the last quad.

## What was not expected of the hardware

Two-input VectorE instructions that do not wait for each other (pieces of 256 columns, 0.335 us apart) held one gather for up to 2.7 us (3.66 less 0.945; 2.3 in the changed kernel) when they followed column-scalar one-hots directly. It happened in iterations 0 to 4 of every such kernel and in iteration 15 of some, and never when VectorE waited for its last one-hot ahead of them or the one-hots had two inputs. In the iterations that run as a loop, where the trace has register instructions of VectorE's sequencer between the pieces, it did not happen once in ten. Why the passage matters, and whether it is these steps that break it, was not tried and stays open.
